# A transformer layer's first and last batch: half-head stacks issued nine to three, batch 1's projections moved inside the scores, the last residual added in PSUM

## The reference, cut to what matters

```python
x = x + attn(layernorm(x))          # qkv = x @ qkv_w.T + b; softmax(q k^T / 4) v; @ proj_w.T + proj_b
x = x + ffn(layernorm(x))           # clip to +-448, round to float8_e4m3, @ weight_fp8.T + bias
```

## Time and profile before

| | us |
|---|---|
| median of 3 runs | 935.46 (935.4 to 943.87) |
| the profiled execution's own time | 935.03 |
| its span in the trace | 933.1 |
| slot 1, step 0 to slot 2, step 0 | 23.58 to 69.48 |
| a slot in the middle (slot 2) | 69.48 to 124.6 |
| the last values' end to the end of the span | 914.6 to 933.1 |

### The profile page before, as it was taken

How to read it: one execution, slowest core, us unless ns; L and a number is a source line. 1 busy time by engine, 2 the same in 40 slices (tenths; PEclk the granted TensorE clock), 3 DMA queues, 4 the chain that set the end, 5 groups by cost and what they waited for, 6 DMA issues and landing times.

```text
span 933.1 us, 17044 instructions
## 1 busy us (share of the span) xinstructions
PE 913.7 (98%) x5894; PEld 433.8 (46%) x5894; DVE 837.7 (90%) x1267; ACT 666.2 (71%) x1291; POOL 513.1 (55%) x528
## 2 busy tenths in 40 slices
PE   7999999999999999999999999999999999998997
PEld 5444444445444454444445454444544444443335
DVE  6978899898989989899998989999898998899976
ACT  3277767777776777777677777777777677776783
POOL 4533448285574928647393764839466482924323
PEclk9999999999999999999999999999999999999999
DMA  7864607456381654718265371835538073560101
GB/s 199 139 102 86 98 25 137 70 77 108 56 141 34 120 70 81 120 46 143 44 107 78 74 133 34 142 56 103 80 64 144 1 141 45 84 100 4 46 24 47
DMA packets 46350, 79.45 MB, mean 85 GB/s; under 512 B 10104, under 2 KB 13304, under 8 KB 46264
## 3 DMA queue, kind: packets, MB, share of 16 engines
q1 hardware_dynamic: 45496, 77.18, 46.8%
q10 hardware_dynamic: 768, 1.18, 0.7%
HBM read 18.42 MB, written 8.39 MB: 29 GB/s over the span
## 4 chain that ended last, share of the span: by engine, by line
PE 93%; DVE 3%; ACT 2%; issue 1%; DMA 0%; POOL 0%; ACTq 0%; DVEq 0%; POOLq 0%
PE ps_t L596 27%; PE ps_o L636 27%; PE ps_m L453 10%; PE ps_s L615 9%; PE ps_m L504 6%; PE ps_m L539 5%; PE ps_m L571 3%; DVE mx L962 2%; PE ps_s L523 1%; PE ps_m L516 1%; ACT pt L759 1%; PE ps_m L554 1%; PE ps_s L475 1%; DMA xin<-in_x 0%; PE ps_s L596 0%
## 5 line engine op out<-in xcount | busy, mean ns | idle before, releaser
L759 ACT ACTIVATE pt<-ps_t 128x512 f32<-128x512 f32 x1008 | 548.8, 599 | 188.8 <-PE ps_t L596 185.0
L962 DVE TENSOR_REDUCE mx<-ps_s 128x2 f32<-128x1024 f32 x512 | 611.6, 1207 | 43.0 <-PE ps_s L615 41.6
L596 PE MATMUL ps_t<-qs,ks 50*128 50x512 f32 x1008 | 375.8, 449 | 6.7 <-ACT pt L759 6.7
L615 PE MATMUL ps_s<-ks,qs 48*128 48x512 f32 x1024 | 375.1, 450 | 0.0
L596 PEld LDWEIGHTS ps_t<-qs,ks 50*128 50x128 f32 x1008 | 159.7, 184 | 285.9 <-ACT pt L759 207.6
L636 PE MATMUL ps_o<-pt,vt 128*32 128x512 f32 x2048 | 272.3, 604 | 0.0
L1291 POOL TENSOR_TENSOR on<-ot,rden 128x256 f32<-128x256 f32 x63 | 39.2, 622 | 226.2 <-DVE rden L1023 226.2
L615 PEld LDWEIGHTS ps_s<-ks,qs 48*128 48x128 f32 x1024 | 158.5, 184 | 6.6 <-DVE mx L962 4.0
L453 PE MATMUL ps_m<-xnT_p,wqkv_p 128*128 128x512 f32 x360 | 109.1, 420 | 0.1
L1282 POOL TENSOR_TENSOR parts<-parts 128x512 f32<-128x512 f32 x60 | 81.7, 1361 | 4.9
L636 PEld LDWEIGHTS ps_o<-pt,vt 128*32 128x32 f32 x2048 | 40.5, 108 | 88.1 <-issue 81.8
(11 more groups left out here) (130 smaller groups left out, 831.4 us busy)
## 6 DMA issues: line engine op xcount, KB each, us to landing
qs<-parts SPq DMA_DIRECT2D x186, 128.0 KB, 4.5
ks<-parts SPq DMA_DIRECT2D x180, 128.0 KB, 5.2
xin<-in_x SPq DMA_DIRECT2D x16, 512.0 KB, 3.6
xres<-in_x SPq DMA_DIRECT2D x16, 512.0 KB, 5.7
out<-h SPq DMA_DIRECT2D x31, 256.0 KB, 2.5
qs<-nmax SPq DMA_DIRECT2D x256, 4.0 KB
pt<-in_qkv_wT SPq DMA_DIRECT2D x1, 768.0 KB, 5.4
qs<-parts SPq DMA_DIRECT2D x12, 64.0 KB, 3.3
```

The source lines that it names most:

```text
L596: nc.tensor.matmul(t_bank(b, s, g), ks[par][rows, slot, keys], qs[par][rows, slot, :], start=True, stop=True).then_inc(st_done, 1)
L615: done = nc.tensor.matmul(ps_s[:, s % 2, g, :], qs[par][rows, slot, queries], ks[par][rows, slot, :], start=True, stop=True)
L759: nc.scalar.activation(pt[n % 2][:, w % 2 + 2 * a, w // 2, :], t_bank(b, s, a), ACT.Exp, scale=SCALE).then_inc(exp_done, 1)
L962: dve.tensor_reduce(mx[:, r, :, s % QUARTER], ps_s[:, s % 2, :, :], AX_X, ALU.max).then_inc(max_done, 1)
```

## The change

What it does, part by part (names of the kernel before unless the diff shows them):

1. Stacks of the first half heads: ScalarE's queue issues three of the first 12 DMAs, Sync nine; Sync then issues the 12 of the second half. The six 128 KB stacks of K's second half of the heads stay on ScalarE's queue but come after its copies in step 2 (`stack_second_k`).
2. TensorE no longer waits for `low_ready` 4 and `v_ready` 4 ahead of step 0; three unread products instead of five, into `ps_o`; batch 1's x is transposed in steps 1 and 2.
3. Batch 1's Q/K projection: two products a step in steps 5 to 16, odd tiles in `ps_o`. `WARM_STEPS` becomes two unread products in steps 0, 3 and 4 and one in step 8. V and x of slot 1 move to steps 22, 24, 26, 28.
4. Batch 2's layer-norm sums move from ahead of the first maximum to steps 15 to 19 of slot 1, and GpSimd applies it after its four splits.
5. Slot 17: the four fill products and the last reload of x are gone. `xin[1]` still holds batch 15's x; GpSimd adds the projection's bias to it at the slot's start, and later forms a second copy with the linear bias.
6. `finish`: the residual is added by two fp32 products with the identity in each token half; VectorE's addition and GpSimd's bias addition go; statistics and mean subtraction read PSUM. TensorE computes attention output + residual + both biases a second time into `ps_o` and `ps_m` (24 fp32r products and four identity products), ScalarE copies it to `h` (`copy_sum`). `FILL_VALUES` goes and `FILL_NORM` is 3 instead of 26.

```diff
-FILL_VALUES = 3
-FILL_NORM = 26
+FILL_NORM = 3
-FILL_STEPS = (2, 4, 6, 8)
-PROJECT_QK_1 = (range(4, 10), range(10, 16), (16, 17), (18, 19))
+PROJECT_QK_1 = ((5, 6, 7), (8, 9, 10), (11, 12, 13), (14, 15, 16))
+TRANSPOSE_X_1 = (1, 2)
+VALUES_AND_X_1 = (22, 24, 26, 28)
+LN1_SUM_1 = (15, 16, 17, 18)
+LN1_END_1 = 19
-WARM_SCORES = 5
-WARM_STEPS = (2, 2, 2, 2, 1, 1, 1, 1, 3, 1, 1, 1, 1, 1, 1, 1)
+WARM_SCORES = 3
+WARM_STEPS = (2, 0, 0, 2, 2, 0, 0, 0, 1)
...
@@ sync, first_slot
-                for half in range(2):
-                    sp.wait_ge(whole_ready, 1)
-                    for r in (0, 1):
-                        copy_first(sp, qs, 0, Q_PARTS, r, half)
-                    sp.wait_ge(low_ready, 1)
-                    copy_first(sp, qs, 0, Q_PARTS, 2, half)
+                sp.wait_ge(whole_ready, 1)
+                for r in (0, 1):
+                    copy_first(sp, qs, 0, Q_PARTS, r, 0)
+                sp.wait_ge(low_ready, 1)
+                copy_first(sp, qs, 0, Q_PARTS, 2, 0)
                 sp.wait_ge(low_ready, 2)
+                copy_first(sp, ks, 1, K_PARTS, 1, 0)
+                copy_first(sp, ks, 1, K_PARTS, 2, 0, (1,))
+                for r in (0, 1, 2):
+                    copy_first(sp, qs, 0, Q_PARTS, r, 1)
...
@@ tensor, finish
-                unread(FILL_VALUES)
+                pe.wait_ge(res_ready, b + 1)
                 for half in range(2):
+                    add_rows(ps_s[:, half], half, res_last)
                     pe.wait_ge(oT_high, NT * b + 2 + half)
...
+                pe.wait_ge(both_ready, 1)
+                for half in range(2):
...
+                    for j in range(2):
+                        column = 2 * half + j
+                        for m, (t, pw, px) in enumerate((t, pw, px) for t in range(NT) for pw, px in PAIRS):
+                            nc.tensor.matmul(sum_bank(half)[:, j, :], oT_p[:, px, t, column * P:(column + 1) * P],
+                                             wproj_p[:, pw, t, :], start=m == 0, stop=False)
+                        last = nc.tensor.matmul(sum_bank(half)[:, j, :], ident[:], xres[:, column, :],
+                                                start=False, stop=True)
+                    last.then_inc(sum_done, 1)
                 unread(FILL_NORM)
...
@@ scalar, stack_k and finish
+                copy_first(act, ks, 1, K_PARTS, 0, 0)
+                copy_first(act, ks, 1, K_PARTS, 2, 0, (0,))
...
+                    if half == 1:
+                        copy_sum(b, 0)
                     act.wait_ge(rs2_ready, b + half + 1)
...
+                copy_sum(b, 1)
...
@@ vector, finish
-                    dve.tensor_tensor(h[:, tok, :], ps_s[:, half, :, 0:D], xres[:, tok, :], ALU.add).then_inc(h_ready, 1)
                     for j in range(2):
-                        ln2_sum(b, 2 * half + j)
+                        dve.bn_stats(st2[:, 2 * half + j, :], ps_s[:, half, j, 0:D]).then_inc(ln2_sums, 1)
```

161 lines of the change are left out of this document (92 added, 69 removed).

## The result

The changed kernel takes 939.34 us (median of 20 runs, 936.59 to 945.17) against 935.11 for the kernel before (20 runs): a ratio of 1.0044, 95% interval 1.0027 to 1.0061. I had predicted 934.1. The profiled execution took 938.06 (span 936.2) where that of before took 935.03. Single executions of the changed kernel spread over 8.6 us, so what follows from one profile holds for that execution; the medians say what is typical.

The account below looks back on a forecast made before the run. TensorE was busy 98% of the span, with VectorE pacing steps 0 to 15 of slot 1. Gains of 0.65 (slot 2), 0.5 (slot 17) and 0.1 (end) made 1.25 us: 933.8, median 934.1; range 933.2 to 934.9.

Parts of the forecast that it names:

- Step 0: Slot 1's first step: starts at 21.9 instead of 23.58 when the twelfth stack lands, gaining 1.7 us (1.0 to 2.2).
- Step 8: Slot 1: waits for the other 12 stacks, now behind nine on Sync; stall 0.6 us (0 to 2.9).
- Step 16: Slot 1: Sync's later issues come at most 1.5 us later, with 18.7 us of cover; costed at nothing.
- ScalarE's second-K stacks: Slot 1: 128 KB stacks beginning over a microsecond later, given as an argument against a stall at step 8.
- Rival 4: Slot 1: thinned steps 17 to 20 drop the clock, slowing steps 21 and 22; 3 us, 936.9, chance 0.06.
- Sums and projections: Slot 1, steps 15 to 28: step 23 comes 0.95 us earlier, 0.3 lost behind it; slot 2 0.65 earlier.
- Slot 17 and the end: Slot 17 without fill products gains 0.5 us (0.4 to 1.0); the end gains 0.1 (0.45 to -0.8).
- the sum: Whole kernel: 1.25 us off the profiled 935.03 gives 933.8; with half of 0.43 kept, a median of 934.1.

Follow-up runs that it names:

- e6: Kernel before with only batch 0's stacks split nine on Sync and three on ScalarE per K half: 944.96 us, ratio 1.0073.
- e9: The same kernel as e6, profiled once more: 936.66 us, a single execution.
- e3: Changed kernel with Sync waiting for the four row copies to land before it issues batch 1's first stacks: 940.52 us, ratio 1.0029.
- e13: Changed kernel with ScalarE's six 128 KB second-K stacks issued right behind the V evictions: 941.20 us, ratio 1.0064.
- e5: Kernel before with only the new end (slot 17 and `finish` as changed): 934.49 us, ratio 0.9968.
- e14: Kernel before with only ScalarE's six second-K stacks held back, issued from about 25.3 us instead of 23.8: 938.24 us, ratio 1.0038.
- e18: e17 with the row copies issued ahead of batch 3's load: 944.15 us, ratio 1.0074.
- e1: Changed kernel with the first twelve stacks again issued six by Sync and six by ScalarE: 947.75 us, ratio 1.0098.
- e17: Changed kernel with stacks, their issuers, transpositions and step 0 as in the kernel before: 944.04 us, ratio 1.0069.
- e7: Changed kernel with row copies ahead of batch 3's load and more unread products before step 0, at step 15 and in steps 17 to 20: 940.43 us, ratio 1.0032.
- e8: Changed kernel with batch 1's projections back at the old steps and the unread products beside them as before: 940.77 us, ratio 1.0055.
- e2: Changed kernel with the four row copies issued ahead of batch 3's load in slot 1: 936.05 us, ratio 1.0002.
- e11: Changed kernel, nine-three split kept, with only step 0 held back to where it was: 937.78 us, ratio 1.0006.
- e12: Kernel before with the new end and batch 1's row copies issued ahead of batch 3's load: 934.14 us, ratio 0.9963.

## Why the prediction was wrong

**Step 0.** Forecast 21.9 (21.1 to 22.6), measured 22.27, with its wait ended by a DMA as written. Gain 1.3 instead of 1.7: right but for 0.4. But nothing was won by it: TensorE came to the wait of step 16 by as much sooner.

**Step 8.** Last stack forecast at 30.6 to 32.0, landed at 31.03. Stall 0.6 forecast, next to none in the profile of the changed kernel: step 8 began at 31.07, 8.80 after step 0 (8.74 before), with 0.04 us in hand. In e6, e9, e3 and e13 it is there with 1.1 to 3.2 us. Right as a danger.

**Step 16: the step that failed.** "What Sync issues after it comes at most 1.5 us later than before and has until step 16; I cost it at nothing, and if that cover is gone, step 16 waits." The issue times were right (the load 31.56 against 30.63, the rows even earlier). What ran was a wait of 4.30 us for the row copies, and 17.1 us at half clock behind it. I compared issues where landings count. I had a DMA share of 0.88 over that stretch in the earlier trace rows and landings that grew, used both for step 8, and then let 18.7 us of time pass for the queue to drain, as if it would. Before, it is full from 27 us on and drains between 37 and 40; in the changed kernel it is still at 1.05 from 38 to 42. Worse, I had no row for when the rows land in the kernel before. The landing events of its trace have it: 40.01, 2.3 us ahead of the need at 42.29. In e5, with the same start, they land at 43.23, and step 16 waits:

```profile
43.28 0.49 PE L602 MATMUL ps_t<-qs,ks 50*128 50x512 f32 x1 [0.94 <-DVE mx L990]
```

The view names VectorE, but the start is 0.05 us behind the landing of the last row copy, so it is the same DMA wait. The cover that one profile shows is not the cover that every execution has. Against e5 the changed kernel's 4.30 us add up: 0.94 that was there already, 1.42 since its need comes at 40.92 and not at 42.34, and 1.95 since its rows land at 45.18 and not at 43.23. The first two need nothing to land later than before.

**ScalarE's second-K stacks.** "ScalarE's 128 KB stacks begin over a microsecond later than before" stood in my text as an argument against a stall. e14 shows that this alone costs 1.9 us by the medians. My own rule, that each instruction of a moved step counts, I had applied to Sync's queue and not to ScalarE's.

**The clock.** Rival 4 had the mechanism (thin steps, then half clock in steps 21 and 22) at a chance of 0.06 and 3 us. The measured 2.46 us between step 16 and slot 2 fit its size, and steps 21 and 22 alone lose 2.8 us; the chance was off. In the changed kernel the clock falls already during the wait of step 16, so there its cause is that wait or the steps ahead of it; e18 and e1 show the thin steps 17 to 20 do it without one. The unread products that the change drops I costed at nothing, as free room beside VectorE's pace: they were 22 in steps 0 to 15 and are 7. e17 against e5 prices such thinning at its worst, 944.04 against 934.49, with the moved projections, sums and V-and-x steps in it. That putting them back would have saved the change is not shown (e7 and e8 didn't). The Trainium skill's "TensorE: Matmul & The Clock Gate", section "HAM oscillation", says that a wait for a DMA drops the clock and that the work behind it starts cold. Step 16 of the changed kernel and of e2 agree (waits of 4.30 and 1.33 us, then 17.1 us at 1.2 GHz each), e5 with its 0.94 us doesn't fall, and e17 falls with no wait for a DMA and none above 0.63 us.

**Sums and projections.** Not visible: the forecast 0.95 us gained at step 23 and 0.3 lost behind it lie under the half clock. Open.

**Slot 17 and the end.** 0.5 and 0.1 forecast, 1.3 together measured, 1.36 in e5. Slot 17 gives 4.57 - 3.97 = 0.60 up to the rounded activations (908.10 against 904.13), and 0.84 up to the end of the last values (918.40, 3.73 late). In the end the mechanism was right (the last part starts behind TensorE's own products), only the term was mis-sized: from the end of the values to the last part I had 10.4 us, from the rows it is 928.50 - 918.40 = 10.10, against 925.21 - 914.67 = 10.54 before: a gain of 0.44 where I had 0.1. One slip in the sum, of no weight: 933.8 and half of 0.43 make 934.0, not 934.1.

**The parts don't add.** By the medians, each against the kernel before on its chip, the split alone costs 9.4 us (6.8 by the ratio), the late second-K stacks 1.9, the thinned steps as e17 has them 8.3, and the whole change, end included, 4.2. The change thins and delays, but it also puts step 0's transpositions into steps 1 and 2 and keeps nine-three with an early step 0 (e1 against the changed kernel: 947.75 against 939.34). e11 has the split too, with thinned steps and a late step 0, and lies only 1.6 above. In what way these pay each other is not settled.

**What beats both.** The new end with the old start: 934.49 (e5), with rows first 934.14 (e12), 1.1 and 2.1 us below the kernel before on their chips.

## What to carry to other kernels

Where a queue's share is near 1, a transfer's slack is the time from its landing to its need, not from its issue, and it must be read for the last transfer of the burst and over several executions. Work that is pulled forward to meet a fixed landing only waits longer. A stretch paced by another engine has no free room on TensorE if unread products stand there: before they go, price the stretch at half clock (in e17 a step went from 1.1 to 1.87 us, since TensorE's two score products and two projections took longer than VectorE's maximum). And look at the mean clock of all executions beside the profile: here the profiled ones were often the better ones.

## What I had not expected of the hardware

Transfers between on-chip buffers in 128 KB stacks kept all engines full (1.07) at 123 to 126 GB/s, while the stretch with the load from memory moved 210 to 213 GB/s at 1.05. Whether that load moves among the stacks or behind them differs between executions with row copies issued at the same times, and moves their landing by 3.2 us (40.01 before, 43.23 in e5). Once fallen, the granted clock stayed at 0.50 for 17.05 us in the changed kernel although TensorE was busy for 13.62 of them, and for 37.5 us in e17, where it was busy nearly all of the time. The clock fell in e17 and e18 with no TensorE wait above 0.63 us. And executions of one kernel differ by up to 12 us (935.25 to 947.61 in e6, at mean clocks of 1.000 to 0.982); that late landings start it is likely from the above, but no slow one of e6 was profiled.
